# Opening of a transformer decoder layer: key list on the mask alone, batch-wise normalisation, query weight on the second queue, query projection in two halves

## The chip, the cores and the metric

The kernel runs on one core of a Trainium2 chip. The metric is the device time of one execution in microseconds, as the median of several runs. A core has five instruction streams that run side by side and wait for each other by semaphores: TensorE (PE; its weight loads are listed as PEld), VectorE (DVE), ScalarE (ACT), GpSimd (POOL) and SyncE (SP). Each takes its instructions in the order in which they are written. SP and ScalarE also issue the transfers; each has a queue of its own to the DMA engines.

## What is computed

One decoder layer on x of 4 batches by 128 tokens by 512 channels: cross-attention to 2048 context keys per batch, self-attention, and a mixture of 8 experts with top-k choice. Each part is added to x.

```python
x = x + _L0_xattn_ref(_layernorm(x, axis=-1), ctx_1024, fside_BxS2_0, mask_BxS2_bk0, ...)
x = x + _L0_attn_ref(_layernorm(x, axis=-1), L0_attn_Wq, ...)
x = x + _L0_ffn_ref(_layernorm(x, axis=-1), L0_ffn_gate_w, ...)
```

Only the first part's beginning is touched. In it

```python
q = (tgt @ Wq_w.T + Wq_b).reshape(b, sq, NUM_HEADS, HEAD_DIM)
k, v = (kv[:, :, 0], kv[:, :, 1])
scores = jnp.einsum('bthd,bshd->bhts', q, k * scale)
scores = scores + attn_bias[:, None, None, :]
pad = jnp.where(memory_key_padding_mask, 0.0, -jnp.inf).astype(scores.dtype)
scores = scores + pad[:, None, None, :]
attn = jax.nn.softmax(scores, axis=-1)
```

`tgt` is the layer-normalised x, `kv` the projection of the context. The mask says which keys count.

## The kernel before

**Chunks of keys.** The 4 x 2048 keys are 64 chunks of 128. A chunk without any key that counts is left out. Which chunks are left is worked out on the chip, at the start, from the mask: VectorE reduces the mask per chunk and computes indices (L659 to L665), TensorE multiplies by a triangle and by a selection (L1112 to L1116), VectorE writes the list as whole numbers into `table` (L677, L678). Every engine reads its loop bound and its chunk numbers from `table`. SP can't issue the first context chunk (L261) before it.

**Normalisation and turning.** For each of the four batches VectorE computes mean and variance (`statistics`, L633 to L635), GpSimd the inverse root (L320), VectorE the normalised batch (L640, `norm`). TensorE transposes it (`turn_batch`, L1085), four 128 by 128 pieces each, into a bank of `ps`. A product with float32 accuracy is made from three products of parts: ScalarE writes the rounded part of the turned batch (`tr_hi`, L412), VectorE the rest (`tr_lo`, L646). The same is done to each weight: ScalarE's `split_att` writes `w_hi`, VectorE's `split_att` writes `w_lo` (L652), 128 by 2048 at a time. The list `SPLITS` gives their order; its first entry is the query weight wq.

**Bias rows.** VectorE makes three bf16 rows of mask and key bias per chunk (`kb_3`, L688 to L694); SP stores them to memory and later loads four copies for each chunk (L275, L268).

**TensorE's order** is written out by hand: four `turn_batch`, the key projection of chunk 0 (L1066, 16 matmuls, each listed as two rows), the query projection of all batches (`project_t`, L1092), the first scores (L1131, L1136), the value projection of chunk 0 (L1076, 12 matmuls), then `chunk(0)` with the key projection of chunk 1, and the loop. The query projection makes 48 matmuls of 512 columns; it goes bank by bank, so that bank g is complete after 12 x (g + 1):

```python
for g in range(KC):
    cols_g = slice(g * P, (g + 1) * P)
    product(dst[g], [(w[:, slot, k, cols_g], t[:, k]) for k in range(KC)
                     for w, t in ((w_hi, tr_hi), (w_lo, tr_hi), (w_hi, tr_lo))]).then_inc(done, 1)
```

**VectorE's order behind it** is fixed too. `queries(c)` takes bank c out of PSUM in two instructions (L721, L722). Other work stands between the four:

```python
queries(0)
dve.wait_ge(in_bo, 16)
for b in range(B):
    ins = v.tensor_tensor(x_s[:, b], x_s[:, b], bo_b[:], ALU.add)
link(ins)
queries(1)
split_att(2)
queries(2)
queries(3)
split_att(3)
```

The first scores wait for all four (`q_out`).

**Transfers at the start.** SP issues the four batches of x, then wq, wk; after the table the first context chunk and wv. ScalarE issues the mask, the key bias (both count on `in_mask`), four columns of biases and the value bias, and later the weights of self-attention.

## Time and profile before

| what | value |
|---|---|
| median of three runs | 493.87 us (492.96 to 494.02) |
| the profiled execution: time | 491.83 us |
| its span, from the first instruction to the last | 489.9 us |
| around the span | 1.9 us |
| PE busy in the span | 434.6 us (89%) |
| VectorE busy | 376.9 us (77%) |
| ScalarE busy | 288.7 us (59%) |
| GpSimd busy | 86.7 us (18%) |
| moved by DMA | 81.95 MB |

The profile is one execution, so its own time is the one to which its durations add up. It is 2.04 us below the median. Busy shares are means over stages of different kinds: the first 12 us have hardly any PE work, the rest nearly nothing else. Ends of matmuls are modelled; the distance of two starts is the better measure of a matmul. Spans of GpSimd are rough. The granted clock of TensorE has two levels in this trace, 1.00 (2.4 GHz) and 0.50 (1.2 GHz); a slice in which it changed has a value between.

### The profile page before, as it was taken

The page shows a single profiled execution, that of the slowest core. Times are in us where ns is not written, and L with a number is a line of the kernel's source. Part 1 is how long each engine was busy: PE and PEld are TensorE (multiplying, and loading weights), DVE is VectorE, ACT ScalarE, POOL GpSimd, SP SyncE. Part 2 cuts the span into 40 slices and gives each one's busy share as a digit, 9 for nine tenths or more (in the row PEclk, how much of TensorE's full clock was granted, in tenths as well). Part 3 has the DMA queues.
Part 4 walks back from the last instruction along what each step waited for, and adds up shares of the span by engine and source line. Part 5 has one row for each costly group of instructions (what it writes and reads, how often), then busy time and mean ns, then how long its engine had stood idle before and what let it go on. Part 6 is the DMA issues. An engine that isn't in the chain of part 4 may idle for free. (4 is left out here: it accounts for less than half of the span.)

```text
span 489.9 us, 9479 instructions
## 1 busy us (share of the span) xinstructions
PE 434.6 (89%) x3262; PEld 358.6 (73%) x3262; DVE 376.9 (77%) x495; ACT 288.7 (59%) x594; POOL 86.7 (18%) x87
## 2 busy tenths in 40 slices
PE   0999999999994689997894599999999999999993
PEld 0878888888883468885773578787878787878782
DVE  4987777766778677556787689889898989898963
ACT  1536666666664312266324277877878787878752
POOL 4010000000005002000006015050505050505000
PEclk9999999999998699999996699999999999999998
DMA  7890000000000390240000049999999999999002
GB/s 256 258 352 25 23 22 22 22 22 22 22 22 0 111 361 3 86 171 3 2 2 0 1 172 387 387 386 388 357 368 305 349 312 369 328 341 327 24 0 86
DMA packets 42956, 81.95 MB, mean 167 GB/s; under 512 B 3000, under 2 KB 3128, under 8 KB 42936
## 3 DMA queue, kind: packets, MB, share of 16 engines
q1 hardware_dynamic: 38744, 75.85, 43.8%
q10 hardware_dynamic: 4192, 5.83, 3.6%
q8 instruction: 13, 0.21, 0.2%
q14 instruction: 7, 0.06, 0.0%
HBM read 80.58 MB, written 1.10 MB: 167 GB/s over the span
## 5 line engine op out<-in xcount | busy, mean ns | idle before, releaser
L1021 DVE TENSOR_TENSOR w_lo<-att_w,w_hi 128x2048 fp32r<-128x2048 f32 x60 | 137.8, 2305 | 22.7 <-ACT w_hi L578 22.7
L578 ACT CAST w_hi<-att_w 128x2048 fp32r<-128x2048 f32 x60 | 115.0, 1917 | 15.4 <-PE po L1359 15.4
L419 ACT ACTIVATE big_a<-ps,negm 128x128 f32<-128x128 f32 x176 | 62.2, 403 | 26.3 <-DVE negm L757 26.3
L1359 PE MATMUL po<-w_hi,ht_hi 128*128 128x512 f32 x128 | 51.8, 405 | 0.0
L1359 PE MATMUL po<-w_hi,ht_lo 128*128 128x512 f32 x128 | 50.6, 395 | 0.0
L1359 PE MATMUL po<-w_lo,ht_hi 128*128 128x512 f32 x128 | 50.5, 394 | 0.0
L1066 PE MATMUL pk<-ctx_s,att_w 128*128 128x128 f32 x352 | 43.0, 282 | 0.0
L419 ACT ACTIVATION_READ_ACCUMULATOR big_a<-ps,negm 128x1 f32 x176 | 43.0, 244 | 0.0
L1066 PEld LDWEIGHTS pk<-ctx_s,att_w 128*128 128x128 f32 x352 | 41.3, 196 | 1.9 <-issue 1.8
L754 DVE TENSOR_REDUCE mc<-ps 128x8 f32<-128x1024 f32 x22 | 26.8, 1219 | 13.2 <-PE ps L1136 13.2
L352 POOL COPY q_now<-qk 128x512 f32 x10 | 7.6, 764 | 119.7 <-PE ps L1136 119.7
L1359 PEld LDWEIGHTS po<-w_hi,ht_lo 128*128 128x128 f32 x128 | 24.1, 188 | 5.7
L1359 PEld LDWEIGHTS po<-w_lo,ht_hi 128*128 128x128 f32 x128 | 24.1, 188 | 5.1
L1359 PEld LDWEIGHTS po<-w_hi,ht_hi 128*128 128x128 f32 x128 | 24.1, 188 | 5.0
L392 POOL CAST back_now<-state 128x128 fp32r (+1 forms) x8 | 8.6, 1074 | 103.3 <-PE ps L1399 87.6
L1359 PE MATMUL pk<-w_hi,xin_hi 128*128 128x512 f32 x64 | 26.2, 410 | 0.3 <-DVE xin_lo L1010 0.3
L1359 PE MATMUL pv<-w_hi,xin_hi 128*128 128x512 f32 x64 | 25.9, 405 | 0.0
L776 DVE COPY big_b<-ps 128x512 f32<-128x512 f32 x33 | 21.8, 685 | 4.8 <-PE ps L1143 4.8
L1359 PE MATMUL pv<-w_hi,xin_lo 128*128 128x512 f32 x64 | 25.3, 395 | 0.0
L1359 PE MATMUL pk<-w_hi,xin_lo 128*128 128x512 f32 x64 | 25.3, 395 | 0.0
L1359 PE MATMUL pv<-w_lo,xin_hi 128*128 128x512 f32 x64 | 25.2, 394 | 0.0
L1359 PE MATMUL pk<-w_lo,xin_hi 128*128 128x512 f32 x64 | 25.2, 394 | 0.0
(274 smaller groups left out, 971.0 us busy)
## 6 DMA issues: line engine op xcount, KB each, us to landing
att_w<-in_w SPq DMA_DIRECT2D x64, 1024.0 KB, 7.4
ctx_s<-in_ctx_t SPq DMA_DIRECT2D x11, 256.0 KB, 2.6
x_s<-in_x SPq DMA_DIRECT2D x4, 256.0 KB, 4.1
att_w<-in_wq SPq DMA_DIRECT2D x1, 1024.0 KB, 9.1
att_w<-in_wk SPq DMA_DIRECT2D x1, 1024.0 KB, 11.8
att_w<-in_wv SPq DMA_DIRECT2D x1, 1024.0 KB, 5.3
att_w<-in_sq ACTq DMA_DIRECT2D x1, 1024.0 KB, 6.9
att_w<-in_wo ACTq DMA_DIRECT2D x1, 1024.0 KB, 8.8
```

Source lines behind the costliest of these rows:

```text
L352: g.tensor_copy(q_now[:], qt[:, bass.ds(b, 1)].rearrange("p a k n -> p (a k) n")).then_inc(q_staged, 1)
L392: g.tensor_copy(back_now[:], back[:, bass.ds(e, 1), :].rearrange("p a n -> p (a n)")).then_inc(back_staged, 1)
L419: ins = a.activation(big_a[:, h], ps[:, c, g * P:(g + 1) * P], ACT.Exp, bias=negm[:, h:h + 1], accum_out=sums[:, h:h + 1])
L578: a.copy(w_hi[:, i % SLOTS], att_w[:, i]).then_inc(hi_ok, 1)
L754: v.tensor_reduce(mc[:, hs], ps[:, 2 * half:2 * half + 2].rearrange("p c (g k) -> p (c g) k", k=P), AX.X, ALU.max).then_inc(loop_dve, 1)
L776: v.tensor_copy(big_b[:, c * KC:(c + 1) * KC].rearrange("p h k -> p (h k)"), ps[:, c]).then_inc(pt_dve, 1)
L1021: v.tensor_tensor(w_lo[:, i % SLOTS], att_w[:, i], w_hi[:, i % SLOTS], ALU.subtract).then_inc(lo_ok, 1)
L1066: ins = mm(pk[:, g * P:(g + 1) * P], wk_s[:, k, g * P:(g + 1) * P], ctx_s[:, k], start=k == 0, stop=k == KC - 1)
L1359: ins = mm(dst, l, r, start=start and i == 0, stop=i == len(terms) - 1, skip_group_check=True)
```

## The change

1. The key bias has a semaphore of its own, `in_kb`. The key list waits for the mask alone (L659); the bias rows wait for `in_kb`.
2. VectorE no longer does all statistics, then all four normalisations, then the low parts. After the first statistics it does the index copy, after the second the table and the first normalisation; then statistics and normalisations alternate, and the low parts of the first two turned batches stand between.
3. wq is loaded by ScalarE's queue, third after mask and key bias and ahead of the columns, and no longer by SP's queue between x and wk.
4. wq leaves `SPLITS`. ScalarE and VectorE split it in two halves of 128 by 1024 (`split_query`), with the second half's high part behind the third turned batch. All waits on the count of split weights go down by one.
5. `project_queries` takes the place of `project_t` for the queries: for all four banks the matmuls of the weight's first half, then for all four those of the second. `q_mm` is counted in the second round only.

```diff
@@ -253,7 +253,6 @@
         def _(sp):
             for b in range(B):
                 sp.dma_start(x_s[:, b], x[b]).then_inc(in_x[b], 16)
-            sp.dma_start(wq_s, wq.rearrange("(k p) n -> p k n", p=P)).then_inc(in_wq, 16)
             sp.dma_start(wk_s, wk.rearrange("(k p) n -> p k n", p=P)).then_inc(in_wk, 16)
             def load_chunk(t):
...
@@ -444,13 +443,21 @@
                 turned_last(t)
             act.dma_start(mask_s[:], key_mask).then_inc(in_mask, 16)
-            act.dma_start(kb_s[:], key_bias).then_inc(in_mask, 16)
+            act.dma_start(kb_s[:], key_bias).then_inc(in_kb, 16)
+
+            def load_att(dst, w, landed):
+                act.dma_start(dst, w.rearrange("(k p) n -> p k n", p=P)).then_inc(landed, 16)
+
+            load_att(wq_s, wq, in_wq)
             for i, v in enumerate((bq, bk, sbq, sbk)):
                 act.dma_start(cols[:, i, :], v).then_inc(in_cols, 16)
             act.dma_start(bv_b[:], bv.partition_broadcast(P)).then_inc(in_cols, 16)
-            def load_att(dst, w, landed):
-                act.dma_start(dst, w.rearrange("(k p) n -> p k n", p=P)).then_inc(landed, 16)
+            def split_query(half):
+
+                ks = slice(2 * half, 2 * half + 2)
+                act.wait_ge(in_wq, 16)
+                a.copy(w_hi[:, 2, ks], wq_s[:, ks]).then_inc(wq_hi_ok, 1)
             def split_chunk(t):
...
@@ -458,21 +465,24 @@
                 act.wait_ge(v_mm, t + 1)
                 a.copy(ctx_hi, ctx_s[:]).then_inc(ctx_hi_ok, 1)
-            split_att(0)
-            for b in range(B):
-                transposed(0, b)
+            transposed(0, 0)
+            transposed(0, 1)
+            split_query(0)
+            transposed(0, 2)
+            split_query(1)
+            transposed(0, 3)
             last = last_chunk(act)
             split_chunk(0)
             act.dma_start(bo_b[:], bo.partition_broadcast(P)).then_inc(in_bo, 16)
             load_att(sq_s, sq, in_sq)
+            split_att(0)
+            load_att(wo_s, wo, in_wo)
             split_att(1)
-            load_att(wo_s, wo, in_wo)
-            split_att(2)
             for dst, w, landed in ((sv_s, sv, in_sv), (sk_s, sk, in_sk), (so_s, so, in_so)):
                 load_att(dst, w, landed)
             act.dma_start(gate_s[:], gate.rearrange("(k p) e -> p k e", p=P)).then_inc(in_gate, 16)
             act.wait_ge(q_mm, KC)
-            split_att(3)
+            split_att(2)
             split_chunk(1)
             softmax_chunk(0, False)
             with act.Fori(1, last) as t:
...
@@ -654,7 +664,7 @@
             def heads(ap):
                 return ap.rearrange("p (g j d) -> p j g d", j=STRIPS, d=DH)
-            dve.wait_ge(in_mask, 32)
+            dve.wait_ge(in_mask, 16)
             dve.wait_ge(consts, 11)
             v.tensor_reduce(idx[:, 3:4], mask_s[:], AX.X, ALU.max)
             link(v.tensor_scalar(idx[:, 2:3], idx[:, 0:1], float(NCH), None, ALU.is_ge))
...
@@ -665,26 +675,33 @@
             v.tensor_tensor(idx[:, 7:8], idx[:, 3:4], idx[:, 6:7], ALU.max).then_inc(act_ok, 1)
             dve.wait_ge(in_x[0], 16)
             statistics(0)
-            dve.wait_ge(in_x[1], 16)
-            statistics(1)
             dve.wait_ge(place_mm, 1)
             link(v.tensor_copy(idx[:, 4:5], pv[0:NJ, 0:1]))
             v.tensor_scalar(pick[:], slots[:], idx[:, 4:5], idx[:, 7:8], ALU.is_equal, ALU.mult).then_inc(pick_ok, 1)
-            dve.wait_ge(in_x[2], 16)
-            statistics(2)
+            dve.wait_ge(in_x[1], 16)
+            statistics(1)
             dve.wait_ge(table_mm, 1)
             n_at = 2 * (NJ + 1)
             v.tensor_copy(table[:, 0:n_at], pv[0:1, 0:n_at]).then_inc(table_ok, 1)
             v.tensor_scalar(table[:, n_at:n_at + 1], pv[0:1, n_at:n_at + 1], -1.0, None, ALU.add).then_inc(table_ok, 1)
-
+            normed_batch(0, 0)
+            dve.wait_ge(in_x[2], 16)
+            statistics(2)
+            normed_batch(0, 1)
             dve.wait_ge(in_x[3], 16)
             statistics(3)
-            for b in range(B):
-                normed_batch(0, b)
-            split_att(0)
-            for b in range(B):
-                transposed(0, b)
-
+            normed_batch(0, 2)
+            transposed(0, 0)
+            normed_batch(0, 3)
+            transposed(0, 1)
+
+            def split_query(half):
+
+                ks = slice(2 * half, 2 * half + 2)
+                dve.wait_ge(wq_hi_ok, half + 1)
+                v.tensor_tensor(w_lo[:, 2, ks], wq_s[:, ks], w_hi[:, 2, ks], ALU.subtract).then_inc(wq_lo_ok, 1)
+
+            dve.wait_ge(in_kb, 16)
             link(v.tensor_scalar(kb_m[:], mask_s[:], 1.0, MASKED, ALU.subtract, ALU.mult))
             link(v.tensor_tensor(kb_m[:], kb_m[:], kb_s[:], ALU.add))
             link(v.tensor_copy(kb_3[:, 0], kb_m[:]))
...
@@ -692,6 +709,11 @@
             link(v.tensor_copy(kb_3[:, 1], kb_m[:]))
             link(v.tensor_tensor(kb_m[:], kb_m[:], kb_3[:, 1], ALU.subtract))
             v.tensor_copy(kb_3[:, 2], kb_m[:]).then_inc(rows_ok, 1)
+            split_query(0)
+            transposed(0, 2)
+            transposed(0, 3)
+            split_query(1)
+
             def v_evacuate(t):
...
@@ -728,10 +750,10 @@
                 ins = v.tensor_tensor(x_s[:, b], x_s[:, b], bo_b[:], ALU.add)
             link(ins)
             queries(1)
-            split_att(2)
+            split_att(1)
             queries(2)
             queries(3)
-            split_att(3)
+            split_att(2)
             last = last_chunk(dve)
             def running(tensor, t):
...
@@ -1099,6 +1121,19 @@
                     product(dst[g], [(w[:, slot, k, cols_g], t[:, k]) for k in range(KC)
                                      for w, t in ((w_hi, tr_hi), (w_lo, tr_hi), (w_hi, tr_lo))]).then_inc(done, 1)
+            def project_queries():
+
+                for half in range(2):
+                    pe.wait_ge(wq_lo_ok, half + 1)
+                    for g in range(KC):
+                        cols_g = slice(g * P, (g + 1) * P)
+                        for k in (2 * half, 2 * half + 1):
+                            for w, t in ((w_hi, tr_hi), (w_lo, tr_hi), (w_hi, tr_lo)):
+                                ins = mm(banks[g], w[:, 2, k, cols_g], t[:, k], start=k == 0 and w is w_hi and t is tr_hi,
+                                         stop=k == KC - 1 and t is tr_lo, skip_group_check=True)
+                        if half:
+                            ins.then_inc(q_mm, 1)
+
             def project(slot, b, dst, done):
                 now = slice(b * T, (b + 1) * T)
...
@@ -1185,11 +1220,10 @@
             pe.wait_ge(in_wk, 16)
             k_project(0)
             pe.wait_ge(tr_lo_ok[0], B)
-            pe.wait_ge(att_lo_ok, 1)
-            project_t(2, banks[0:4], q_mm)
+            project_queries()
             pe.wait_ge(q_out, 4)
             scores(0)
-            pe.wait_ge(att_lo_ok, 2)
+            pe.wait_ge(att_lo_ok, 1)
             for k in range(KC):
                 v_project(0, k)
             chunk(0, False)
```

VectorE at the beginning, before: all four normalisations in one piece, behind them the weight, the low parts (`tr_lo`) and the bias rows.

```order
L677 CAST table<-pv 1x130 [waits table_mm]
L678 TENSOR_SCALAR table<-pv 1x1
L633 BN_STATS stats<-x_s 128x6 [waits in_x3]
L634 BN_AGGR aggr<-stats 128x2 [waits dchain]
L635 TENSOR_SCALAR rstd<-aggr 128x1 [waits dchain]
L640 TENSOR_SCALAR norm<-x_s,aggr,rstd 128x512 [waits rstd_ok] x4
L652 TENSOR_TENSOR w_lo<-att_w,w_hi 128x2048 [waits att_hi_ok]
L646 TENSOR_TENSOR tr_lo<-ps,tr_hi 128x4x128 [waits tr_hi_ok0] x4
L688 TENSOR_SCALAR kb_m<-mask_s 64x128
```

VectorE at the same place now. Line numbers are those of the changed file: L650 is the normalisation, L656 the low part, L643 the statistics.

```order
L685 CAST table<-pv 1x130 [waits table_mm]
L686 TENSOR_SCALAR table<-pv 1x1
L650 TENSOR_SCALAR norm<-x_s,aggr,rstd 128x512 [waits rstd_ok]
L643 BN_STATS stats<-x_s 128x6 [waits in_x2]
...
L650 TENSOR_SCALAR norm<-x_s,aggr,rstd 128x512 [waits rstd_ok]
L643 BN_STATS stats<-x_s 128x6 [waits in_x3]
...
L650 TENSOR_SCALAR norm<-x_s,aggr,rstd 128x512 [waits rstd_ok]
L656 TENSOR_TENSOR tr_lo<-ps,tr_hi 128x4x128 [waits tr_hi_ok0]
L650 TENSOR_SCALAR norm<-x_s,aggr,rstd 128x512 [waits rstd_ok]
L656 TENSOR_TENSOR tr_lo<-ps,tr_hi 128x4x128 [waits tr_hi_ok0]
L705 TENSOR_SCALAR kb_m<-mask_s 64x128 [waits in_kb]
...
L702 TENSOR_TENSOR w_lo<-att_w,w_hi 128x1024 [waits wq_hi_ok]
```

The table and the first normalisation moved ahead of the third statistics, the fourth normalisation behind the low part of the first batch; the weight's low part is cut in two and the bias rows come before it.

TensorE where the query projection meets the first scores, before: L1066 is the key projection, L1092 the query projection (12 matmuls for each bank in a row, of which the first three and the last are shown), L1131 the start of the scores.

```order
L1066 MATMUL pk<-ctx_s,att_w 128x128 [waits ctx_in,in_wk]
L1066 MATMUL pk<-ctx_s,att_w 128x128 x15
L1092 MATMUL ps<-tr_hi,w_hi 128x512 [waits att_lo_ok,tr_lo_ok0]
L1092 MATMUL ps<-tr_hi,w_lo 128x512
L1092 MATMUL ps<-tr_lo,w_hi 128x512
...
L1092 MATMUL ps<-tr_lo,w_hi 128x512
L1131 MATMUL ps<-bias,ones 128x512 [waits q_first,k_out,bias_in,q_out]
```

TensorE at the same place now: L1088 is the key projection, L1132 the query projection (its first matmul, its 24th and 25th and its last are shown), L1166 the start of the scores.

```order
L1088 MATMUL pk<-ctx_s,att_w 128x128 [waits ctx_in,in_wk]
L1088 MATMUL pk<-ctx_s,att_w 128x128 x15
L1132 MATMUL ps<-tr_hi,w_hi 128x512 [waits wq_lo_ok,tr_lo_ok0]
...
L1132 MATMUL ps<-tr_lo,w_hi 128x512
L1132 MATMUL ps<-tr_hi,w_hi 128x512 [waits wq_lo_ok]
...
L1132 MATMUL ps<-tr_lo,w_hi 128x512
L1166 MATMUL ps<-bias,ones 128x512 [waits q_first,k_out,bias_in,q_out]
```

The first matmul waits for half of the weight's low part, the matmul after 24 for the other half. The number of matmuls is the same, 48; what moved is that each bank gets its last matmul in the second 24.

VectorE behind the query projection now. L743 and L744 are `queries`, L750 the output bias added to x, L662 the low part of a weight.

```order
L732 TENSOR_TENSOR kt_s<-pk,cols 128x512 [waits k_mm,in_cols]
L743 TENSOR_SCALAR q_now<-ps,cols 128x128 [waits q_mm]
L744 TENSOR_SCALAR qk<-ps,cols 128x4x128
L750 TENSOR_TENSOR x_s<-x_s,bo_b 128x512 [waits in_bo]
L750 TENSOR_TENSOR x_s<-x_s,bo_b 128x512 x3
L743 TENSOR_SCALAR q_now<-ps,cols 128x128 [waits q_mm,dchain]
L744 TENSOR_SCALAR qk<-ps,cols 128x4x128
L662 TENSOR_TENSOR w_lo<-att_w,w_hi 128x2048 [waits att_hi_ok]
L743 TENSOR_SCALAR q_now<-ps,cols 128x128 [waits q_mm]
L744 TENSOR_SCALAR qk<-ps,cols 128x4x128
L743 TENSOR_SCALAR q_now<-ps,cols 128x128 [waits q_mm]
L744 TENSOR_SCALAR qk<-ps,cols 128x4x128
```

Here nothing moved against the kernel before: the same instructions stand in the same order between the first evacuation and the last.

## Rows read from the trace of the kernel before

**Rows 1.** Waits, 0 to 50 us: engine, tile, line, releaser: us, times, longest.

```profile
PE ps L1131 <- DVE qk L722: 1.1, 1, 1.1
```

**Rows 2.** Timeline, VectorE's query evacuations: start, us, engine, line, op, operands, count.

```profile
24.23 0.33 DVE L721 TENSOR_SCALAR q_now<-ps,cols 128x128 f32<-128x128 f32 x1
...
25.14 2.48 DVE L728 TENSOR_TENSOR x_s<-x_s,bo_b 128x512 f32<-128x512 f32 x4
...
28.58 2.28 DVE L652 TENSOR_TENSOR w_lo<-att_w,w_hi 128x2048 fp32r<-128x2048 f32 x1
...
32.81 0.74 DVE L722 TENSOR_SCALAR qk<-ps,cols 128x512 f32<-128x512 f32 x1
```

**Rows 3.** Timeline of PE, 13 to 33 us.

```profile
13.15 3.67 PE L1085 MATMUL ps<-ident,norm 128*128 128x128 f32 x16 [2.10 <-DVE norm L640]
...
16.62 4.73 PE L1066 MATMUL pk<-ctx_s,att_w 128*128 128x128 f32 x32
...
21.10 0.48 PE L1092 MATMUL ps<-tr_hi,w_hi 128*128 128x512 f32 x1
...
32.10 0.40 PE L1092 MATMUL ps<-tr_lo,w_hi 128*128 128x512 f32 x1
```

**Rows 4.** Timeline of the beginning, 3 to 21 us (in brackets: idle before, releaser).

```profile
3.31 0.51 SPq L257 DMA_DIRECT2D att_w<-in_wk  x1
...
4.25 0.14 POOL L344 MEMSET neg_max<- 128x64 f32 x1
...
6.71 0.28 DVE L659 TENSOR_REDUCE idx<-mask_s 64x1 f32<-64x128 uint8 x1 [6.59 <-DMA kb_s<-in_key_bias]
...
11.50 0.14 DVE L678 TENSOR_SCALAR table<-pv 1x1 int32<-1x1 f32 x1
...
12.56 1.91 DVE L640 TENSOR_SCALAR norm<-x_s,aggr,rstd 128x512 f32<-128x512 f32 x4
...
13.17 0.36 SPq L261 DMA_DIRECT2D ctx_s<-in_ctx_t  x1
...
14.38 2.29 DVE L652 TENSOR_TENSOR w_lo<-att_w,w_hi 128x2048 fp32r<-128x2048 f32 x1
...
16.58 2.48 DVE L646 TENSOR_TENSOR tr_lo<-ps,tr_hi 128x512 fp32r<-128x512 f32 x4
...
20.82 0.68 DVE L705 TENSOR_TENSOR w_lo<-ctx_s,w_hi 128x512 fp32r<-128x512 f32 x1
```

**Rows 5.** Timeline, chunk 0 after the first scores.

```profile
41.43 0.69 DVE L710 TENSOR_TENSOR kt_s<-pk,cols 128x512 f32<-128x512 f32 x1 [0.27 <-PE pk L1066]
```

**Rows 6.** DMA issues, 0 to 80 us: count, KB each, median us to landing.

```profile
ctx_s<-in_ctx_t SPq DMA_DIRECT2D x6, 256.0 KB, 2.6
...
att_w<-in_wk SPq DMA_DIRECT2D x1, 1024.0 KB, 11.8
...
mask_s<-in_key_mask ACTq DMA_DIRECT2D x1, 8.0 KB, 2.8
```

**Rows 7.** Stretch: us, PE, PEld, DVE, ACT, POOL busy, clock, DMA share, GB/s.

```profile
13.00:14.50 1.50, 1.35 (x7) 1.35 (x8) 1.50 (x5) 1.04 (x2) 0.59 (x1) 1.00 0.36 97
```

**Rows 8.** Slices of 1 us: PE busy (instructions), granted clock, DMA share, GB/s.

```profile
152.00:153.00 1.00, 0.73 (x28) 1.00 0.00 0
...
155.00:156.00 1.00, 0.00 (x0) 0.61 0.00 0
...
163.00:164.00 1.00, 0.00 (x1) 0.50 0.00 0
...
168.00:169.00 1.00, 1.00 (x4) 0.56 0.85 283
...
223.00:224.00 1.00, 0.00 (x0) 1.00 0.00 0
...
273.00:274.00 1.00, 0.00 (x0) 0.50 0.00 0
...
278.00:279.00 1.00, 1.00 (x10) 0.95 0.00 0
```

More of the change, by code:

```diff
@@ L165, in decoder_layer @@
         rows3 = nc.dram_tensor("rows3", [NJ, 3, P], BF16, kind="Internal").ap()
-        in_mask, in_wk, in_wv, in_bo, in_sb, in_gate, in_cols = (sem(f"in_{n}") for n in (
-            "mask", "wk", "wv", "bo", "sb", "gate", "cols"))
+        in_mask, in_kb, in_wk, in_wv, in_bo, in_sb, in_gate, in_cols = (sem(f"in_{n}") for n in (
+            "mask", "kb", "wk", "wv", "bo", "sb", "gate", "cols"))
         in_wq, in_wo, in_sq, in_sk, in_sv, in_so = (sem(f"in_{n}") for n in ("wq", "wo", "sq", "sk", "sv", "so"))
-        att_hi_ok = sem("att_hi_ok"); att_lo_ok = sem("att_lo_ok")
+        wq_hi_ok = sem("wq_hi_ok"); wq_lo_ok = sem("wq_lo_ok"); att_hi_ok = sem("att_hi_ok"); att_lo_ok = sem("att_lo_ok")
         in_x = [sem(f"in_x{b}") for b in range(B)]
@@ L289, in _ @@
             sp.wait_ge(v_mm, last + 2)
-            sp.wait_ge(att_lo_ok, 4)
+            sp.wait_ge(att_lo_ok, 3)
             for i in range(2 * NQ):
@@ L294, in _ @@
                 if i == 5:
+                    sp.wait_ge(att_lo_ok, 5)
+                if i == 6:
                     sp.wait_ge(att_lo_ok, 6)
-                if i == 6:
-                    sp.wait_ge(att_lo_ok, 7)
                 sp.dma_start(att_w[:, i], w_tile(0, i)).then_inc(raw_in[i], 16)
@@ L494, in _ @@
                 transposed(2, b)
-            act.wait_ge(att_lo_ok, 5)
-            split_att(5)
+            act.wait_ge(att_lo_ok, 4)
+            split_att(4)
             for c in range(KC):
@@ L713, in _ @@
             split_chunk(0)
-            split_att(1)
+            split_att(0)
             dve.wait_ge(in_cols, 80)
@@ L879, in _ @@
             values_out(2)
-            split_att(5)
+            split_att(4)
             for c in range(KC):
@@ L1229, in _ @@
             turn_batch(1, 3)
-            pe.wait_ge(att_lo_ok, 5)
+            pe.wait_ge(att_lo_ok, 4)
             values_project(0)
@@ L1240, in _ @@
             pe.wait_ge(v2_out, B - 1)
-            pe.wait_ge(att_lo_ok, 6)
+            pe.wait_ge(att_lo_ok, 5)
             project_t(0, banks[0:4], k2_mm)
```

14 lines of the change are left out of this document (7 added, 7 removed).

## Prediction

> **What bounds the kernel now.** I read the busy shares first. PE has most of them, but the change touches only the stretch before the loop over chunks, so what counts is which chain sets the moment at which that loop gets going. Everything after it (the other chunks, self-attention, experts) waits for its predecessor and moves with it; a delay there is a delay at the end, one for one.
>
> The waits of the first 50 us come next. The last wait before the first scores is PE's: it stands still for 1.1 us until VectorE has written the last query [rows 1]. The timeline then gives the chain backwards. The scores need the four query evacuations, the last ending at 32.81 + 0.74 = 33.55 [rows 2]; that one waits for the last of 48 projection matmuls, which begin at 21.10, with the last start at 32.10 [rows 3]; these wait for the key projection (16.62 to about 21.1) and it for the transposes that begin at 13.15 [rows 3]. The transposes wait for the normalised batches, these for the whole VectorE list from 6.71 on, and that first instruction waits for the transfer of the key bias [rows 4]. After the first scores PE works without a pause up to 41.4, when VectorE takes over the second key projection after waiting 0.27 us for it [rows 5]. So at 41.4 PE sets the pace, and what it hangs on is 33.55.
>
> **What the change removes at the front.** The key list needs the mask alone: landed at 0.85 + 2.8 = 3.65 [rows 6]. The other thing it waits for is GpSimd's last constant, at 4.25 + 0.14 = 4.39 [rows 4]. So VectorE starts near 4.46 and not at 6.71, 2.25 us earlier. From there I add up its list in the new order with the old durations, all from [rows 4]: index steps and four statistics, with the copies between them, 12.56 - 6.71 = 5.85; a normalisation (14.38 - 12.56)/4 = 0.455; a low part of a turned batch 2.48/4, about 0.6; the four of these with the bias split 20.82 - 16.58 = 4.24; half a weight's low part (16.58 - 14.38)/2 = 1.10. The table was written at 11.50 + 0.14 = 11.64; now VectorE is 2.25 earlier and one statistics step (12.56 - 11.64, about 0.9) fewer stands ahead: about 8.4. The fourth batch is normalised at 4.46 + 5.85 + 3 x 0.455 + 0.6 = 12.3, done 12.8. The last low part of a turned batch is done at 4.46 + 5.85 + 1.82 + 4.24 + 1.10 = 17.5; the second half of the query weight follows at 18.6, long before it is used. GpSimd's four inverse roots and ScalarE's copies lie beside this: each is ready before VectorE gets to it (a root took 0.6 us, a statistics step 0.9).
>
> **PE's side.** Four transposes take 4 x (16.62 - 13.15)/16 = 0.87 [rows 3], so PE could begin the key projection at 12.8 + 0.9 = 13.7 instead of 16.62. It also needs the context chunk and the key weight. The key weight, issued at 3.31, landed 11.8 us later at 15.1, and the chunk, issued at 13.17, 2.6 us later at 15.8 [rows 4, 6]. Now SP issues the chunk 3.2 us earlier, at 8.4 + (13.17 - 11.64) = 9.9 [rows 4], but it stands behind the key weight on SP's queue. Bounds: 13.7, if taking the query weight off SP's queue brings the key weight forward far enough, and 15.8, if nothing changes. I take 14.4, nearer to the low end, because between 13.0 and 14.5 the engines moved only 97 GB/s [rows 7]: most of the key weight was in by 13. The Trainium skill, DMA: Bandwidth & Descriptors, section Issuing engines are not separate DMA queues, speaks against more: transfers issued by different engines run on the same 16 DMA engines and interleave, so issuing from two saves only issue time. By that rule alone the key weight would be as late as before and the start would be 15.4 or so, which adds 1.0 us to the sum; no row of before shows two large loads on the two queues at once at this place.
>
> How long the key projection takes depends on TensorE's pace. In the trace its 32 rows took 4.45 us [rows 3]: about 9 at the 0.217 us of the transposes and 23 at 0.11, so the pace doubled near 18.6, 5.4 us after steady work began at 13.15. (The granted clock is listed as 1.00 there, the pace says otherwise.) Twice later the clock came back from 0.50 to 1.00: at 168.9 after work that resumed at 164.0, and at 278.1 after work that resumed at 274.0 [rows 8]. That is 5.4, 4.9 and 4.1 us of steady work, on average 4.8. The new transposes come one by one with PE idle between them, so I count from 14.4: the pace doubles at 19.2, after 22 slow rows; 10 fast ones add 1.1. **Query projection starts at 20.3** (before: 21.1). It could be 17.5 at the earliest (VectorE's low parts) and 22.0 at the latest (15.8, the pace doubling 5.4 us later, 7 fast rows). So of 2.25 us saved in front, 0.8 is left.
>
> **The two halves.** Here the change loses. Before, bank 0 was complete after 12 of 48 matmuls, and VectorE took the queries over one by one while PE went on. Now every bank is complete only in the second half, the first after matmul 30. A matmul takes (32.10 - 21.10)/47 = 0.234 us, so the first query is ready 30 x 0.234 + 0.3, that is 7.3 us, after the start: at 27.6 (before: at 24.2). Behind it on VectorE stand, in unchanged order, the first query (25.14 - 24.23 = 0.91), the output bias added to x and the second query together (28.58 - 25.14 = 3.44), the low part of the self-attention query weight (2.20), the third query (0.93, as the second) and the fourth (1.0 until it is written) [rows 2, 4]. That is 8.5 us. Before, most of it lay under the projection, which lasted until 32.5; now it begins 3.7 us before the projection ends. **The last query is out at 27.6 + 8.5 = 36.1, not at 33.55: 2.55 us later.** The break-even is a start at 33.55 - 15.8 = 17.75, which is almost the earliest start possible. PE, done at 20.3 + 11.3 = 31.6, stands still until 36.1: 4.5 us instead of 1.1.
>
> **What the longer pause costs.** Nothing else takes it up: the scores, the value projection and the next key projection are PE's and follow it. VectorE's low part of the next weight ends 2.2 us after the fourth query, as before, inside the scores and the value projection. In the trace, PE stopped at 152.7 and the clock was at 0.50 by the middle of the slice 155 to 156 [rows 8]: less than 3 us of idleness were enough. A pause of 4.5 us should do the same. After it the half pace lasts about as long as in the three cases above, 4.8 us less whatever of it falls in the pause, and half of that is lost: 2.3 us; bounds 0 (the clock holds) and 3. Chunk 0 has no slack for it on PE.
>
> The rest is free: the key rows are written some 5 us earlier but needed only by the scores; the value weight and the later loads on ScalarE's queue move forward 1 to 3 us and all have their users later; the two extra half splits cost two instructions. The query weight on ScalarE's queue landed at about 12 before; ScalarE reaches it at about 12.1 and the third and fourth turned batch stand behind it, so 2 us of delay there would still hide under the key projection.
>
> **Sum:** 2.55 + 2.3 = 4.85 on the profiled execution, 491.83 + 4.85 = 496.7. The runs' median, 493.87, lies 2.04 above the profiled one, so the median I predict is 498.7.
>
> **The rivals.**
> 1. The clock holds through the pause. For it: PE stood from 222.05 to 224.1 and the clock stayed at 1.00 [rows 8], so some pauses are survived. Then only the later queries count: 491.83 + 2.55 + 2.04 = 496.4; with a start between 18.6 and 22.0, 494.7 to 498.1.
> 2. Not slower: the weights arrive early and the isolated transposes already count as steady work, so that the pace doubles at 15 or 16 and VectorE's low parts at 17.5 set the start. Then the last query is out at 33.3, PE's pause is as long as in the forecast, but with the clock holding the result is -0.25: 493.6. It decides at a start before 18.7, where the loss is under 1 us. Against it: 17.5 is a floor, so no real gain can come of it; and in the trace the pace doubled 5.4 us after work that had no gaps in it. A gain over 1 us would need a start before 16.8, which the durations of VectorE exclude unless several are wrong.
> 3. The load on the second queue competes with x, so that statistics wait too. The third and fourth batch are wanted at about 8.8 and 10.2. Before, the statistics never waited for x, and nothing large ran beside it. Each us of lateness beyond that adds one: 499.7 and more.
> 4. The rule on the queues holds and nothing of the key weight moves forward: the start is at 21.3 and the median 499.7. This lies inside the forecast's own range.
>
> **How the numbers follow.** The forecast (clock falls, at a cost of 1.2 to 3.0, start between 18.6 and 22.0, rival 4 among it) has 0.62, with 495.9 to 501.1 as its own range; rival 1 has 0.20, rival 2 0.12 (of which 0.09 is no change and 0.03 a gain), rival 3 0.06. 0.2% is 1.0 us, about what a measurement of this kernel can tell from no change. Rival 1 at its low end adds 0.02 of no change; 0.01 more goes to a gain by something that I don't see. So faster 0.04, same 0.11, slower 0.85. The range 494.7 to 501.0 leaves out most of rival 2 and the tails of the others.
>
> **What would show it.** In the new profile: the first key-list instruction near 4.5; the context chunk issued near 10; the first matmul of the query projection near 20.3 (right or wrong step on weights and pace); the first query evacuation 7.3 us after it; no wait of VectorE between the four evacuations; PE waiting some 4.5 us before the first scores; value-projection matmuls at about twice the 0.23 us of before after that, and a granted clock of 0.50 for some of it. It would be wrong if VectorE's list were not in this order, if the projection began before 18, or if loop and pace swallowed the delay.

## The result and the profile after

The changed kernel is slower: 497.68 us in the median of 19 runs against 493.52 of 19 runs of the kernel before; ratio 1.0087, 95% interval 1.0067 to 1.0108, so +4.2 us (+3.3 to +5.3). Its profiled execution took 499.47 us, 1.8 over its median, with a span of 497.6 us; that of before, 491.83, is 1.7 below the median of its 19 runs (2.04 below that of the first three), so the difference of the two profiles' spans, 7.7 us, is larger than the one of the medians and has to be taken apart.

The page of the changed kernel, PE's busy time and its granted clock in 40 slices:

```profile
span 497.6 us, 9481 instructions
...
PE 440.9 (89%) x3262; PEld 362.6 (73%) x3262; DVE 377.5 (76%) x496; ACT 288.6 (58%) x595; POOL 85.9 (17%) x87
...
PEclk9997999999999599998997599999999999999998
```

PE is busy 6.3 us longer with the same 3262 matmuls: some of them ran slower. The digit 7 in the fourth slice (37 to 50 us) is new.

Timeline of the changed kernel, the beginning. These rows answer to [rows 3, 4]:

```profile
4.50 0.28 DVE L669 TENSOR_REDUCE idx<-mask_s 64x1 f32<-64x128 uint8 x1 [4.39 <-POOL neg_max L343]
...
8.29 0.14 DVE L686 TENSOR_SCALAR table<-pv 1x1 int32<-1x1 f32 x1
...
9.97 0.36 SPq L260 DMA_DIRECT2D ctx_s<-in_ctx_t  x1
...
12.60 0.54 DVE L650 TENSOR_SCALAR norm<-x_s,aggr,rstd 128x512 f32<-128x512 f32 x1
...
15.81 5.29 PE L1088 MATMUL pk<-ctx_s,att_w 128*128 128x128 f32 x32 [1.51 <-DMA ctx_s<-in_ctx_t]
...
20.85 0.48 PE L1132 MATMUL ps<-tr_hi,w_hi 128*128 128x512 f32 x1
```

VectorE starts 2.2 us earlier, the table is written and the chunk issued 3.2 us earlier. Then the gain goes: PE waits for the chunk until 15.81 and starts the key projection there (before: at 16.62, straight behind its transposes), and the query projection starts at 20.85 (before: 21.10).

The query evacuations, answering to [rows 2]:

```profile
28.11 0.35 DVE L743 TENSOR_SCALAR q_now<-ps,cols 128x128 f32<-128x128 f32 x1 [4.97 <-PE ps L1132]
...
29.03 2.49 DVE L750 TENSOR_TENSOR x_s<-x_s,bo_b 128x512 f32<-128x512 f32 x4
...
32.48 2.28 DVE L662 TENSOR_TENSOR w_lo<-att_w,w_hi 128x2048 fp32r<-128x2048 f32 x1
...
35.86 0.74 DVE L744 TENSOR_SCALAR qk<-ps,cols 128x512 f32<-128x512 f32 x1
...
36.66 0.61 PE L1166 MATMUL ps<-bias,ones 32*128 32x512 bf16 x4 [4.42 <-DVE qk L744]
```

VectorE stands idle for 4.97 us ahead of the first query and from then on is never idle up to the last, which it ends at 36.60 (before: 33.55). PE waits 4.42 us for it (before: 1.1 [rows 1]).

PE's granted clock by slices of 1 us in that pause and after it (busy, instructions, clock, DMA), a row's counterpart being [rows 8]:

```profile
35.00:36.00 1.00, 0.00 (x0) 0.99 0.13 25
36.00:37.00 1.00, 0.34 (x4) 0.50 0.00 0
...
42.00:43.00 1.00, 1.00 (x4) 0.60 0.00 0
```

The timeline of chunk 0 shows what it costs; the last row answers to [rows 5]:

```profile
40.79 0.63 PE L1098 MATMUL pv<-w_lo,w_hi 128*128 128x512 f32 x1
41.21 0.63 PE L1098 MATMUL pv<-w_hi,w_lo 128*128 128x512 f32 x1
...
43.11 0.40 PE L1098 MATMUL pv<-w_lo,w_hi 128*128 128x512 f32 x1
43.34 0.39 PE L1098 MATMUL pv<-w_hi,w_lo 128*128 128x512 f32 x1
...
47.34 0.69 DVE L732 TENSOR_TENSOR kt_s<-pk,cols 128x512 f32<-128x512 f32 x1 [1.88 <-PE pk L1088]
```

The clock fell to 0.50 when the pause was almost over, 0.7 us before PE resumed, and came back in the slice 42 to 43. Starts are 0.42 us apart until then and 0.23 after. The key evacuation is at 47.34 and not at 41.43: 5.9 us, of which 36.60 - 33.55 = 3.05 are the later queries and 2.86 the clock. After the loop over the chunks the delay is the same (first turned output 158.97 before, 164.90 after). The other 1.8 us of the difference between the spans come from another place:

```profile
230.00:231.00 1.00, 0.33 (x4) 0.77 0.00 0
231.00:232.00 1.00, 1.00 (x24) 0.50 0.00 0
...
233.00:234.00 1.00, 1.00 (x28) 0.52 0.00 0
```

Here, at the first scores of self-attention behind a wait of 2.06 us, the clock fell for 3.4 us; in the profile of before, with the same wait, it held [rows 8, slice 223 to 224]. Nine of the twelve profiles below show this fall too (all but those of e1, e2 and e4), also of kernels that are not slower, so it isn't the change's doing.

### The profile page after: what moved, and what is told of

Read it like the earlier page. It is cut to its first block and busy times, and to the rows that moved or that the text cites. A ratio compares the mean times of both kernels' runs of the same rounds, so it can differ in the third digit from the quotient of the medians.

```text
span 497.6 us, 9481 instructions
## 1 busy us (share of the span) xinstructions
PE 440.9 (89%) x3262; PEld 362.6 (73%) x3262; DVE 377.5 (76%) x496; ACT 288.6 (58%) x595; POOL 85.9 (17%) x87
## 5 line engine op out<-in xcount | busy, mean ns | idle before, releaser
L588 ACT CAST w_hi<-att_w 128x2048 fp32r<-128x2048 f32 x60 | 115.0, 1917 | 15.4 <-PE po L1393 15.4
L1088 PE MATMUL pk<-ctx_s,att_w 128*128 128x128 f32 x352 | 43.6, 284 | 1.5 <-DMA ctx_s<-in_ctx_t 1.5
L1088 PEld LDWEIGHTS pk<-ctx_s,att_w 128*128 128x128 f32 x352 | 41.7, 198 | 3.7 <-issue 3.7
L351 POOL COPY q_now<-qk 128x512 f32 x10 | 6.1, 613 | 128.2 <-PE ps L1171 128.2
## 6 DMA issues: line engine op xcount, KB each, us to landing
att_w<-in_wk SPq DMA_DIRECT2D x1, 1024.0 KB, 11.6
```

What stands on the lines that cost most here:

```text
L351: g.tensor_copy(q_now[:], qt[:, bass.ds(b, 1)].rearrange("p a k n -> p (a k) n")).then_inc(q_staged, 1)
L588: a.copy(w_hi[:, i % SLOTS], att_w[:, i]).then_inc(hi_ok, 1)
L1088: ins = mm(pk[:, g * P:(g + 1) * P], wk_s[:, k, g * P:(g + 1) * P], ctx_s[:, k], start=k == 0, stop=k == KC - 1)
```

## The experiments

The theory: (a) ordering the matmuls by halves makes the first query late, and the work that stands between the evacuations on VectorE then lies open; (b) the longer pause of PE lets the clock fall; (c) what the front saves is nearly lost at the chunk's transfer. The rival for (a) is that something else in the beginning loses the time, for (b) that PE has slack in chunk 0. All ratios are against the kernel before on the same chip.

| run | ratio, 95% interval | projection starts | last query out | key evacuation, chunk 1 |
|---|---|---|---|---|
| before | 1 | 21.10 | 33.55 | 41.43 |
| changed | 1.0087, 1.0067 to 1.0108 | 20.85 | 36.60 | 47.34 |
| e1 | 1.0011, 0.9983 to 1.0039 | 20.48 | 32.97 | 40.87 |
| e2 | 1.0087, 1.0059 to 1.0115 | 18.96 | 34.73 | 44.19 |
| e3 | 0.9985, 0.9955 to 1.0015 | 20.85 | 33.30 | 41.18 |
| e4 | 1.0073, 1.0047 to 1.0099 | 18.87 | 34.62 | 42.54 |
| e5 | 1.0109, 1.0073 to 1.0145 | 20.28 | 36.05 | 45.48 |
| e6 | 1.0048, 1.0022 to 1.0073 | 20.81 | 36.56 | 43.08 |
| e7 | 1.0009, 0.9985 to 1.0033 | 20.85 | 33.30 | 40.84 |
| e8 | 1.0068, 1.0045 to 1.0092 | 20.84 | 36.62 | 44.51 |
| e9 | one run, 491.12 us | 18.44 | 30.87 | 38.79 |
| e10 | 1.0047, 1.0021 to 1.0072 | 22.80 | 35.24 | 45.01 |
| e11 | 1.0003, 0.9978 to 1.0029 | 20.33 | 32.78 | 40.31 |
| e12 | 1.0010, 0.9979 to 1.0041 | 20.82 | 33.26 | 41.15 |

The three times are of one profiled execution each. They differ between executions of one kernel: in e2's profile the key bias happened to land 1.4 us earlier than in that of before, and its projection starts 2.1 us earlier. So inside a profile the distances count, and the time of the kernel is read from the ratio. From the projection's start to the key evacuation it is 20.3 us in before, e3, e9 and e12 and 20.4 in e1, 23.7 in e4 and e8, 25.2 in e2 and e5, 26.5 in the changed kernel.

### e1: bank by bank again

```diff
-            project_queries()
+            pe.wait_ge(wq_lo_ok, 2)
+            project_t(2, banks[0:4], q_mm)
```

> The changed kernel, with one part undone: the query projection goes bank by bank again, 12 matmuls each, after both halves of the weight's low part. Start of the projection as in the changed kernel, about 20.9 us in its profile. Theory (the halves make the query evacuations late, and the pause that follows lowers the clock): the first query is taken over at about 24.0, the last is out near 33.4 as in the kernel before (33.55), PE waits about 1.1 us before the first scores, no slice near 36 to 42 us at a granted clock of 0.50; time within 0.5 us of the kernel before, 4 to 5 us under the changed kernel. Rival (the loss comes from elsewhere in the beginning, such as the load of the query weight on the other queue or the later value weight): still 3 us or more over the kernel before.

Measured 493.02 us, ratio 1.0011. Timeline of e1, first scores and key evacuation:

```profile
33.03 0.40 PE L1166 MATMUL ps<-bias,ones 32*128 32x512 bf16 x4 [1.11 <-DVE qk L744]
...
40.87 0.69 DVE L732 TENSOR_TENSOR kt_s<-pk,cols 128x512 f32<-128x512 f32 x1 [0.28 <-PE pk L1088]
```

The pause is 1.11 us again and the loss is gone, with everything else of the change in place. So the front, the second queue and the split weight neither cost nor gain anything that a time can show. The rival falls. Nor did the order by halves have anything to gain here: it lets the projection begin on half of the weight, but in the changed kernel the second half's low part was done at 19.03, ahead of the projection's start at 20.85.

### e2: the halves alone

```diff
-            project_t(2, banks[0:4], q_mm)
+            project_halves()
```

`project_halves` is `project_queries` without its waits for the halves; the rest is the kernel before.

> The kernel before, with one part of the change alone: the 48 query matmuls are ordered by halves, all else as before. Theory: projection starts at 21.1, first query taken over at 28.4, last out at 36.9 (21.1 + 7.3 + 8.5), PE waits 4.4 us, the clock falls, and chunk 0 ends 5.5 to 6 us later than in the kernel before; time 3.5 to 5.5 us over the kernel before, that is the whole loss of the changed kernel or a little more. Rival (the halves cost nothing by themselves): within 1 us of the kernel before.

Measured 497.49 us, ratio 1.0087: the whole loss. Timeline of e2:

```profile
34.79 0.39 PE L1143 MATMUL ps<-bias,ones 32*128 32x512 bf16 x4 [4.38 <-DVE qk L722]
...
44.19 0.69 DVE L710 TENSOR_TENSOR kt_s<-pk,cols 128x512 f32<-128x512 f32 x1 [1.88 <-PE pk L1066]
```

From the projection's start to the last query it took 34.73 - 18.96 = 15.8 us, before 12.45. The expected times of day (36.9) were missed, since everything began earlier in this execution; the distances up to the last query are as expected. From the projection's start to the key evacuation it is 25.2 us against 20.3 before, so 4.9 us more and not the 5.5 to 6 that I expected: the fall of the clock cost 1.6 us in this execution and 2.9 in the changed kernel's.

### e3: VectorE's other work ahead of the queries

```diff
+            dve.wait_ge(in_bo, 16)
+            for b in range(B):
+                ins = v.tensor_tensor(x_s[:, b], x_s[:, b], bo_b[:], ALU.add)
+            link(ins)
+            split_att(1)
             queries(0)
-            dve.wait_ge(in_bo, 16)
-            for b in range(B):
-                ins = v.tensor_tensor(x_s[:, b], x_s[:, b], bo_b[:], ALU.add)
-            link(ins)
             queries(1)
-            split_att(1)
             queries(2)
```

> The changed kernel, with VectorE's additions of the output bias to x and the low part of the self-attention query weight moved ahead of the four query evacuations, into the 5 us in which VectorE waits there in the changed kernel's profile (23.1 to 28.1). PE's order is unchanged, halves included. Theory (it is the order on VectorE that makes the halves late): evacuations follow the projection bank by bank, the last is out about 1.0 us after the last matmul, near 33.4; PE waits about 1.1 us, the clock holds; time within 1 us of the kernel before. Rival (a late first bank is enough to lose): last query still near 36, time near the changed kernel's 497.7.

Measured 492.53 us, ratio 0.9985, not different from before. Timeline of e3:

```profile
33.36 0.40 PE L1166 MATMUL ps<-bias,ones 32*128 32x512 bf16 x4 [1.11 <-DVE qk L744]
...
41.18 0.69 DVE L732 TENSOR_TENSOR kt_s<-pk,cols 128x512 f32<-128x512 f32 x1 [0.26 <-PE pk L1088]
```

The projection starts at 20.85 as in the changed kernel, is ordered by halves, and the first query comes at 28.11, as there; yet the last is out at 33.30. It is not the halves in themselves that lose, it is 4.7 us of other work between evacuations that now start late. Either cure, e1 or e3, takes back all of it.

### e4, e8 and e5: the pause filled

```diff
             project_queries()
+            for _ in range(18):
+                mm(po[:, 0], tr_hi[:, 0, 0:P], tr_lo[:, 0], start=True, stop=True, skip_group_check=True)
```

The 18 products are not used. e4 and e8 are the same kernel, e5 is the changed kernel, beside e8 on one chip.

> The changed kernel, with 18 additional matmuls of 512 columns behind the query projection, whose result nobody uses; they take about 18 x 0.234 = 4.2 us of the 4.4 us in which PE waits for the queries, and delay nothing. Theory (part of the loss is the clock that falls in the pause): the last query is out as late as in the changed kernel (36.6), the first scores start there, but no slice up to 50 us is at 0.50; the key projection of chunk 1 ends 2.5 to 2.9 us earlier than in the changed kernel, and the time is 1.5 to 3 us under it, so 1.5 to 3 us over the kernel before. Rival (the clock costs nothing here, PE has slack in chunk 0): the time stays that of the changed kernel.

> The changed kernel unchanged, on the same chip as the next three, to have their differences free of the chip. Both theories: 4 to 4.5 us over the kernel before, granted clock at 0.50 for part of the stretch 34 to 44 us.

> The kernel of e4 again (18 additional matmuls in the pause), now beside the changed kernel on one chip. Theory: the clock's share of the loss is the difference to e5, 1 to 3 us; what stays over the kernel before is 2.5 to 3.5 us, the later queries. Rival (the clock costs nothing): no difference to e5.

Timeline of e8 (the filler, the first scores, the key evacuation):

```profile
32.12 4.28 PE L1225 MATMUL po<-tr_lo,tr_hi 128*128 128x512 f32 x18
36.67 0.39 PE L1166 MATMUL ps<-bias,ones 32*128 32x512 bf16 x4 [0.27 <-DVE qk L744]
...
44.51 0.69 DVE L732 TENSOR_TENSOR kt_s<-pk,cols 128x512 f32<-128x512 f32 x1 [1.30 <-PE pk L1088]
```

and of e5:

```profile
36.10 0.61 PE L1166 MATMUL ps<-bias,ones 32*128 32x512 bf16 x4 [4.38 <-DVE qk L744]
...
45.48 0.69 DVE L732 TENSOR_TENSOR kt_s<-pk,cols 128x512 f32<-128x512 f32 x1 [1.87 <-PE pk L1088]
```

From the last query to the key evacuation it takes 7.88 us in before, 7.89 in e8 and 7.92 in e4, but 9.43 in e5, 9.46 in e2 and 10.74 in the changed kernel. PE computes more in e8 and is faster: the clock's price is 1.55 to 2.86 us in these traces, and none when PE has something to do. The rival, PE having slack there, falls. PE's granted clock by slices of 1 us around the fall, in e5 and then in e2:

```profile
36.00:37.00 1.00, 0.90 (x16) 0.52 0.00 0
...
39.00:40.00 1.00, 1.00 (x5) 0.78 0.01 2
```

```profile
34.00:35.00 1.00, 0.21 (x4) 1.00 1.05 400
35.00:36.00 1.00, 1.00 (x36) 0.85 0.61 141
36.00:37.00 1.00, 1.00 (x10) 0.50 0.00 0
...
39.00:40.00 1.00, 1.00 (x6) 0.94 0.00 0
```

Behind pauses of the same length the clock fell at different moments: 0.7 us before PE resumed in the changed kernel, just as it resumed in e5, 0.9 us after in e2. It stayed at 0.50 for 6.8 us in the changed kernel and for 3.4 in e5 and e2, and half of the time that PE worked in it is about the price.

In the times, e8 (495.94) is 2.9 us under e5 (498.88), its neighbour on one chip: e8's twelve runs lie between 495.3 and 498.2, e5's six between 497.3 and 500.0, and resampling them gives a 95% interval of 1.6 to 3.6 us for the difference of the medians. e4, on another chip, is only 1.4 under the changed kernel. e5 itself is 6.3 us over before where 4 to 4.5 were expected, but with six runs its ratio (1.0073 to 1.0145) holds the 1.0087 of the 19. What stays in e4 and e8, 3.3 to 3.6 us over before, is the later queries (2.55 forecast, 3.05 in the profile; 3.3 if it is counted from the projection's start).

### e6: the value projection in the pause

```diff
+            pe.wait_ge(att_lo_ok, 1)
+            for k in range(KC):
+                v_project(0, k)
             pe.wait_ge(q_out, 4)
             scores(0)
-            pe.wait_ge(att_lo_ok, 1)
-            for k in range(KC):
-                v_project(0, k)
             chunk(0, False)
```

> The changed kernel, with the 12 matmuls of chunk 0's value projection moved ahead of the wait for the queries, so into PE's pause. Theory (PE sets the pace of chunk 0 and the clock falls in the long pause): they run from about 32.1 to 34.9, the pause left is 1.7 us and the clock holds; the scores start at 36.6 as before, the second key projection follows at 37.9 instead of 43.6 and VectorE takes it over at about 41.7 (changed kernel 47.3, kernel before 41.4): time 4 to 5 us under the changed kernel, within 1 us of the kernel before. Rival (VectorE sets the pace of chunk 0): gain of under 2 us against the changed kernel, since the last query is no earlier.

Measured 495.82 us, ratio 1.0048: 1.9 us under the changed kernel's median and 3.1 under e5 on the same chip, where I expected 4 to 5. Timeline of e6:

```profile
36.48 2.28 DVE L662 TENSOR_TENSOR w_lo<-att_w,w_hi 128x2048 fp32r<-128x2048 f32 x1
36.62 0.40 PE L1166 MATMUL ps<-bias,ones 32*128 32x512 bf16 x4 [1.69 <-DVE qk L744]
...
38.68 1.22 DVE L776 TENSOR_REDUCE mc<-ps 128x8 f32<-128x1024 f32 x1
...
42.92 0.50 PE L1098 MATMUL pv<-w_hi 128*128 128x512 f32 x1 [1.25 <-DVE w_lo L727]
...
43.08 0.68 DVE L732 TENSOR_TENSOR kt_s<-pk,cols 128x512 f32<-128x512 f32 x1
```

The pause is 1.69 us and the clock holds, as expected. But the evacuation comes at 43.08 and not at 41.7: it is not waiting for PE any more (no bracket), PE waits 1.25 us for VectorE. The low part of the output weight (36.48 to 38.68) keeps VectorE from the maxima, and 4.4 us of VectorE's own work follow. In e8, the changed kernel without the fallen clock, VectorE waits only 1.30 us for PE at this place (0.27 in before): PE can gain no more than that before VectorE sets the pace. My expectation took PE as the only pace-setter. Here the rival was half right.

### e7, e11 and e10: a kernel better than both?

e7 is e3 with the edit of e6. e11 is e3 with half of the value projection (`v_project(0, 0)`, `v_project(0, 1)`) ahead of the wait and half behind the scores. e10 is e11 with the low part of the output weight on GpSimd:

```diff
-            with pool.Fori(1, last + 1) as t:
+            def stage_query(t):
...
+            stage_query(1)
+            pool.wait_ge(att_hi_ok, 3)
+            g.tensor_tensor(w_lo[:, 2], wo_s, w_hi[:, 2], ALU.subtract).then_inc(att_lo_ok, 1)
+            with pool.Fori(2, last + 1) as t:
+                stage_query(t)
...
             queries(3)
-            split_att(2)
```

> The kernel of e3 (evacuations together), and the value projection of chunk 0 ahead of the wait for the queries as in e6. Theory: last query out near 33.4, value projection to 34.9, scores 34.9 to 36.2, second key projection done at 39.9; now VectorE is the later one in chunk 0 (its low part of the output weight ends at 36.3, the key evacuation follows 4.5 us after, at about 40.9 against 41.4 before): time 0 to 1 us under the kernel before. Rival (PE alone sets the pace): the gain is the whole 1.4 us by which PE is earlier, or more.

> As e10, but the low part of the output weight stays on VectorE ahead of the first maxima. Theory (VectorE sets the pace of chunk 0 once PE's pause is used): first maxima at 36.4 as in e7, key evacuation near 40.8, scores of chunk 1 near 45.5, time 0 to 1 us under the kernel before, and 1 us or so above e10. Rival (PE alone sets the pace): as fast as e10.

> The kernel of e3 with two more moves: PE does half of chunk 0's value projection (6 matmuls, 1.4 us) while it waits for the queries and half after the scores; the low part of the output weight goes from VectorE (2.2 us ahead of the first maxima) to GpSimd, behind its first copy of the queries. Theory (in e6 and e7 VectorE with this low part sets the pace of chunk 0, in e3 PE does): scores near 33.4, maxima at 34.7 and not at 36.7, second key projection done at 39.8, scores of chunk 1 at 44.2 against 45.99 before: 1 to 2 us under the kernel before. Rival (GpSimd's work slows VectorE or holds up its own copy for the next scores): scores of chunk 1 or 2 wait for GpSimd, and time is no better than the kernel before.

e7 measured 493.08 us (1.0009), e11 492.98 (1.0003): not different from before. In both VectorE sets the pace: it takes the key projection over without having waited for PE. From the projection's start to the key evacuation it is 19.99 us in e7 and 19.98 in e11, against 20.33 in before. So both move the evacuation forward by 0.3 us, less than the times can show, and it makes no difference how much of the value projection stands in the pause; that e11's clock time (40.31) is earlier than e7's (40.84) comes from its start. Timeline of e7:

```profile
34.96 0.39 PE L1166 MATMUL ps<-bias,ones 32*128 32x512 bf16 x4
...
40.84 0.68 DVE L732 TENSOR_TENSOR kt_s<-pk,cols 128x512 f32<-128x512 f32 x1
```

e10 was slower, 496.16 us, ratio 1.0047. Timeline of e10:

```profile
16.61 6.43 PE L1093 MATMUL pk<-ctx_s,att_w 128*128 128x128 f32 x32 [2.57 <-DMA ctx_s<-in_ctx_t]
...
37.59 4.53 POOL L355 TENSOR_TENSOR w_lo<-att_w,w_hi 128x2048 fp32r<-128x2048 f32 x1
...
38.26 3.88 DVE L784 SCALAR_TENSOR_TENSOR negm<-mc,neg_max 128x8 f32<-128x8 f32 x1 [0.16 <-DVE mc L781]
```

A 128 by 8 instruction of VectorE, 0.17 us elsewhere, took 3.88 us and ended when GpSimd's 128 by 2048 subtraction did. The low part that VectorE would have done in 2.2 us stopped it for 3.7. This was the rival of the expectation. From the last query to the key evacuation it takes 9.77 us in e10 and 7.53 in e11, 2.2 us more; the medians of the two differ by 3.2. It also lets PE stand for 2.9 us in chunk 0, and in this profile the clock fell at 46.0, behind that wait and 1.1 us after PE had resumed at 44.9, for 3.4 us.

### e9 and e12: the query weight back on SP's queue

e9 and e12 are the same kernel, e3 with one edit:

```diff
+            sp.dma_start(wq_s, wq.rearrange("(k p) n -> p k n", p=P)).then_inc(in_wq, 16)
             sp.dma_start(wk_s, wk.rearrange("(k p) n -> p k n", p=P)).then_inc(in_wk, 16)
...
-            load_att(wq_s, wq, in_wq)
```

> The kernel of e3, with the query weight's load back on SP's queue, between x and the key weight; the early key list, the table and everything else stay. It asks what the change of queue does for the key projection's start, which waits for the first context chunk. If the change of queue gives nothing: the key projection starts between 14.3 and 15.8, as in the seven profiles with the query weight on ScalarE's queue (15.8, 15.2, 15.3, 14.3, 14.7, 15.4, 15.4, 15.6). If it brought the key weight and the chunk forward: it starts at 16.5 or later. Time within 1 us of e3 in either case, since the loss does not hang on it.

> The kernel of e9 (evacuations together, query weight's load on SP's queue), timed. In its one profile the key projection started at 14.9 and ran at full pace from the start, so that the scores of chunk 1 came at 43.4 against 45.99 before; in the profiles of the other variants the pace doubled only at 16 to 19 us. If that came from the queue (x lands undisturbed and the transposes follow each other closer), the time is 1 to 2.5 us under the kernel before. If it was chance of the clock and of the transfers in that execution, the time is that of e3: within 1 us of the kernel before.

Timelines, e9 and then e12:

```profile
14.88 3.81 PE L1088 MATMUL pk<-ctx_s,att_w 128*128 128x128 f32 x32 [0.85 <-DMA ctx_s<-in_ctx_t]
```

```profile
15.62 5.45 PE L1088 MATMUL pk<-ctx_s,att_w 128*128 128x128 f32 x32 [1.59 <-DMA ctx_s<-in_ctx_t]
```

The start is 14.9 and 15.6, inside the 14.3 to 16.6 of the ten profiles with the weight on ScalarE's queue. So no gain by the change of queue shows; a shift well below that spread of 2.3 us would not be seen in two profiles. e9's one run, 491.12 us, looked like a gain: its key projection ran at full pace throughout (3.81 us for 32 rows, 5.45 in e12), which is most of the 2.4 us by which its key evacuation comes ahead of e3's. The timed repetition gave 493.56 us, ratio 1.0010. It was chance. e2, with the order of before, shows the same 3.81 us.

## Why the prediction was right

**The sign, the place and the size** were right: 498.7 forecast, 497.7 measured, inside the range. The chances put 0.85 on slower. The mechanism, late queries and then a fall of the clock, is the one that e1 to e5 and e8 show. That the sum came out so near is partly luck, as two of the points below say.

**VectorE's list.** Forecast: start 4.46, table 8.4, chunk issued 9.9, fourth batch done 12.8. Measured: 4.50, 8.43, 9.97, 13.14. The last one is 0.3 us late, 0.18 of it a wait for the fourth batch of x, the beginning of rival 3 without its consequence.

**The chunk's landing** is a step that was wrong. I took 14.4 between 13.7 and 15.8, because the DMA engines moved only 97 GB/s from 13.0 to 14.5. In the changed kernel they moved 382 in the same stretch, and the chunk took 5.7 us from issue:

```profile
13.00:14.50 1.50, 1.30 (x6) 0.71 (x4) 1.40 (x6) 1.08 (x2) 0.00 (x0) 1.00 1.05 382
```

```profile
ctx_s<-in_ctx_t SPq DMA_DIRECT2D x1, 256.0 KB, 5.7
```

The hole in the old trace was not spare room ahead of the chunk; it goes with the moment at which SP issues the next transfers. The kernel before issued them from 13.17 on and has the hole up to 14.5; e2, which issued them from 11.79 on, has it from 12 to 13 (223 GB/s); the changed kernel and e12, which issued them at 10.0, moved 382 and 401 from 13.0 to 14.5. The key weight landed at 2.83 + 11.6 = 14.4, 0.7 us earlier than before, the chunk behind it at 15.7, and the start was 15.81. The rule of the Trainium skill that I set beside it (DMA: Bandwidth & Descriptors, section Issuing engines are not separate DMA queues) gave 15.4 in my estimate and was nearer. By it the other queue brings nothing forward, and e9 and e12 agree with that within their spread.

**The pace** was off to the other side. I counted 4.8 us of steady work from the start of the key projection; the pace doubled at 18.9, 3.1 us after it. One of the three cases behind the 4.8 was also misread: the work from 164.0 on was not steady, PE was busy for only 0.31 of the slice 165 to 166. The two errors nearly cancelled, which was luck: projection at 20.3 forecast, 20.85 measured. The profiles with the same front have it anywhere from 18.87 (e4) to 22.80 (e10).

**The halves.** Forecast 7.3 us from the start to the first query and 8.5 to the last: measured 28.11 - 20.85 = 7.26 and 36.60 - 28.11 = 8.49. e1, e2 and e3 show that the loss lies in this and nothing else of the change. The delay of the last query, 3.05 against 2.55, is larger by the error in the start. One reading beside it was wrong without harm: the low part of the next weight ended 3.2 us after the fourth query before, because VectorE waited 0.92 us for ScalarE (34.47 + 2.29 against 33.55), and not 2.2. In the changed kernel it is 2.2, and that is the reserve of 1.30 instead of 0.27 us that e6 uses up.

**The pause.** 4.5 us forecast, 4.42 measured, and the clock fell at its end. Its cost was forecast as 2.3 with bounds 0 and 3; the traces have 2.86, 1.55 and 1.58 (changed, e5, e2), and e4 and e8 show that it is the pause that causes it. The 2.3 lies between the two values that occur and is neither. The sum of the two terms, 4.85, stands against 5.9 in the changed kernel's profile and against 4.2 (3.3 to 5.3) in the medians. The medians don't test its second term cleanly. I added it to a profile of before in which the clock held in self-attention, together with the 2.04 us up to the median; but the runs' mean clocks say that the kernel before often has a fall of that length too. Beside e1, its ten runs with a mean clock of 0.965, that of the profile, took 489.9 to 491.8 us, and fourteen with 0.961 took 492.0 to 494.3, the median among them. The changed kernel's median run has 0.962, its profiled one 0.955. So the two median runs have about the same time at the low clock, and the clock's share in 4.2 us is not shown; e8 against e5 is the comparison that shows it in the times.

**Rivals.** Rival 1 (clock holds, 496.4) is what e4 and e8 bring about by their filler: 496.3 and 495.9, or 3.6 and 3.4 us over before where the rival had 2.55. Rival 2 needed a start of the projection before 18.7. Such starts occur, 18.44 in e9 and nearly in e4 (18.87), but the two profiles of the changed kernel have 20.85 and 20.28; and of its 19 runs none is under 496.7.

## What to carry to other kernels

Reordering a product so that all its outputs are completed in the last part saves nothing for a producer that has all its inputs when it starts, and takes away the time in which a consumer on another engine could have done its other work between them; look at what stands in the consumer's list between the first and the last output before doing it. A longer wait of TensorE can cost more than its length, since the clock may fall in it; moving that other work of the consumer ahead of the first output is a cure (e3), as good here as the old order of the product (e1). A saving at the head of a chain is worth only what the next transfer behind a full queue lets through.

## What the runs showed of the hardware that I had not expected

- While GpSimd ran a 4.5 us subtraction, an instruction of VectorE on 128 by 8 values took 3.88 us instead of 0.17 (e10, one profile). There GpSimd was no free place for VectorE's work beside a short chain on VectorE.
- The same wait of 2.06 us in self-attention left the clock at 1.00 in one execution and lowered it to 0.50 for 3.4 us in another, which costs about 1.7 us, half of it. The 19 runs of the kernel before differ by up to 6.3 us.
- The clock can fall after PE has resumed: 0.9 us after in e2, 1.1 us after in e10.
- The first context chunk, issued at 10.0 in all of them, let PE start anywhere between 14.3 and 16.6 us in ten profiles with the query weight on ScalarE's queue, and at 14.9 and 15.6 in two with it on SP's: the spread is larger than the 0.8 us by which the changed kernel starts earlier than before (15.81 against 16.62).
